# Expert weights split into two parts on GpSimd during the batches instead of in the closing stage

## The reference: what is computed

```
x = x + tanh(g_xattn) * attention(layernorm(x), ctx, ctx, Wq, bq, Wk, bk, Wv, bv, Wo, bo)   # 16 heads of 32
probs = softmax(layernorm(x) @ router_w + router_b)                                        # 8 experts
gate, idx = max(probs), argmax(probs)
x = x + tanh(g_ffn) * gate * (layernorm(x) @ expert_w[idx] + expert_b[idx])
```

## Time and profile before

| what | value |
|---|---|
| timed runs, us | 1054.35, 1055.9, 1056.93 (median 1055.9) |
| the profiled execution: its time / its span | 1057.68 / 1056.0 us |
| busy: TensorE, ScalarE, VectorE, GpSimd | 978.0, 811.9, 745.6, 262.0 us |
| mean granted TensorE clock | 0.976 of full speed |
| HBM read, written | 50.42 MB, 18.66 MB |

### The profile page before, as it was taken

How to read it: one execution, slowest core, us unless ns; L and a number is a source line. 1 busy time by engine, 2 the same in 40 slices (tenths; PEclk the granted TensorE clock), 3 DMA queues, 4 the chain that set the end, 5 groups by cost and what they waited for, 6 DMA issues and landing times.

```text
span 1056.0 us, 18686 instructions
## 1 busy us (share of the span) xinstructions
PE 978.0 (93%) x5208; PEld 641.8 (61%) x5208; DVE 745.6 (71%) x1653; ACT 811.9 (77%) x1913; POOL 262.0 (25%) x318
## 2 busy tenths in 40 slices
PE   3798999999999999999999999999999997698996
PEld 2564467656765676567656765676567545576775
DVE  5745655875787578757875787578757778797664
ACT  3688988898889888978898889888988988233431
POOL 6002200430042004200420042004201006454663
PEclk9799999999999999999999999999999989799999
DMA  6334223532443245324532453244325259144542
GB/s 213 97 90 114 79 64 98 143 85 69 115 137 89 69 110 140 89 60 117 136 81 70 117 137 84 68 116 137 86 69 132 62 166 378 56 135 137 163 138 75
DMA packets 70884, 119.37 MB, mean 113 GB/s; under 512 B 17854, under 2 KB 18878, under 8 KB 70656
## 3 DMA queue, kind: packets, MB, share of 16 engines
q1 hardware_dynamic: 64544, 99.49, 34.0%
q0 software_dynamic: 6240, 18.68, 5.5%
HBM read 50.42 MB, written 18.66 MB: 65 GB/s over the span
## 4 chain that ended last, share of the span: by engine, by line
PE 69%; ACT 10%; DVE 7%; issue 6%; DMA 3%; POOL 2%; SPq 2%; DVEq 1%; ACTq 0%; POOLq 0%
PE jb L489 11%; PE jb L490 10%; PE jb L491 10%; PE jb L532 10%; PE sc L512 9%; PE hb L522 9%; PE sc L673 6%; ACT jb L707 5%; ACT probs L695 3%; DVE maxima L819 1%; DVE e_lo L836 1%; PE hb L659 1%; PE jb L603 1%; SPq L452 1%; DMA q_stack<-q_lo 1%
## 5 line engine op out<-in xcount | busy, mean ns | idle before, releaser
L819 DVE TENSOR_REDUCE maxima<-jb 128x1 f32<-128x512 f32 x512 | 335.7, 686 | 112.0 <-PE jb L532 109.5
L707 ACT ACTIVATE jb<-jb,maxima 128x512 f32<-128x512 f32 x512 | 341.9, 678 | 41.4 <-DVE maxima L819 38.0
L695 ACT ACTIVATE probs<-sc 128x512 f32<-128x512 f32 x512 | 284.4, 605 | 40.7 <-PE sc L512 29.2
L532 PE MATMUL jb<-k_stack,q_stack 96*128 96x512 f32 x512 | 207.6, 434 | 24.4 <-ACT jb L707 10.1
L512 PE MATMUL sc<-q_stack,k_stack 98*128 98x512 f32 x512 | 183.9, 423 | 2.8 <-ACT probs L695 1.8
L532 PEld LDWEIGHTS jb<-k_stack,q_stack 96*128 96x128 f32 x512 | 95.9, 191 | 109.1 <-ACT jb L707 59.1
L522 PE MATMUL hb<-probs,values 128*32 128x512 f32 x1024 | 138.8, 616 | 1.0 <-ACT probs L695 0.7
L512 PEld LDWEIGHTS sc<-q_stack,k_stack 98*128 98x128 f32 x512 | 94.1, 191 | 67.9 <-ACT probs L695 36.6
L707 ACT ACTIVATION_READ_ACCUMULATOR jb<-jb,maxima 128x1 f32 x512 | 113.2, 221 | 0.0
L1104 POOL TENSOR_TENSOR stage<-stage,gbo 128x512 f32<-128x512 f32 x31 | 39.8, 1284 | 253.8 <-DMA stage<-in_x 253.8
L1096 POOL TENSOR_TENSOR row<-rt,tiny 128x2 f32<-128x2 f32 x15 | 12.7, 848 | 259.5 <-DVE rt L901 259.5
(11 more groups left out here) (228 smaller groups left out, 1740.3 us busy)
## 6 DMA issues: line engine op xcount, KB each, us to landing
k_stack<-k_hi SPq DMA_DIRECT2D x256, 64.0 KB, 2.0
q_stack<-q_hi SPq DMA_DIRECT2D x256, 64.0 KB, 2.0
stage<-in_x SPq DMA_DIRECT2D x63, 256.0 KB, 3.0
stage<-in_ctx_t SPq DMA_DIRECT2D x32, 256.0 KB, 3.2
k_stack<-k_lo SPq DMA_DIRECT2D x128, 64.0 KB, 2.0
q_stack<-q_lo SPq DMA_DIRECT2D x128, 64.0 KB, 2.0
e_lo<-in_ew SPq DMA_DIRECT2D x8, 1024.0 KB, 10.8
rows<-row SPq DMA_DIRECT2D x30, 257.5 KB, 3.4
```

The costliest lines, as they stand in the source:

```text
L532: nc.tensor.matmul(jbs[j][:], q_stack[g % 2][0:MAXROW, n * P:(n + 1) * P], k_stack[g % 2][0:MAXROW, h * S:(h + 1) * S], start=True, stop=T ...
L695: nc.scalar.activation(probs[:, kt % 2, h, :], scs[(16 * g + n) % NSC][:], ACT.Exp)\
L707: nc.scalar.activation(jbs[j][:], jbs[j][:], ACT.Exp, bias=maxima[g % 2][:, n:n + 1], accum_out=row_sums[g % 2][:, n:n + 1]).then_inc(s["m ...
L819: nc.vector.tensor_reduce(maxima[g % 2][:, n:n + 1], jbs[j][:], AX.X, ALU.max, negate=True)\
```

## The change

Each of the 32 chunks (an expert's 128 x 512 rows) is loaded, split and stored during batches 0 to 6 by GpSimd, five chunks a batch, through two pairs of buffers in `late_room`, a tile that is otherwise used only in the opening and at the end. Both parts are kept in two DRAM tensors. At the end SyncE loads low parts (W) and high parts (H) finished; the ScalarE, VectorE and GpSimd items W are gone.

```diff
+    ew_parts = [nc.dram_tensor(f"ew_{part}", [E, P, NF, D], F32, kind="Internal").ap() for part in ("hi", "lo")]
...
+        x_raw, x_hi = ([late_room[:, (2 * i + m) * S:(2 * i + m + 1) * S] for i in range(2)] for m in range(2))
...
# GpSimd, PER_BATCH = 5, CHUNKS = 32
+                elif kind == "XL":
+                    i = PER_BATCH * t + n
+                    if i < CHUNKS:
+                        if i < 2:
+                            wait(pool, s["w_lo_done"], 3 * NF)
+                        wait(pool, x_out[i % 2], 32 * (i // 2))
+                        nc.gpsimd.dma_start(x_raw[i % 2], ew[i // NF, i % NF * P:(i % NF + 1) * P, :]).then_inc(x_in[i % 2], 16)
+                elif kind == "XS":
...
+                        pool.wait_ge(x_in[i % 2], 16 * (i // 2 + 1))
+                        nc.gpsimd.tensor_copy(x_hi[i % 2].bitcast(F32R), x_raw[i % 2]).then_inc(s["x_hi"], 1)
+                        pool.wait_ge(s["x_hi"], i + 1)
+                        nc.gpsimd.tensor_tensor(x_raw[i % 2].bitcast(F32R), x_raw[i % 2], x_hi[i % 2], ALU.subtract)\
+                            .then_inc(s["x_lo"], 1)
+                elif kind == "XO":
...
+                        pool.wait_ge(s["x_lo"], i + 1)
+                        nc.gpsimd.dma_start(ew_parts[0][i // NF, :, i % NF, :], x_hi[i % 2]).then_inc(x_out[i % 2], 16)
+                        nc.gpsimd.dma_start(ew_parts[1][i // NF, :, i % NF, :], x_raw[i % 2]).then_inc(x_out[i % 2], 16)
# SyncE: W takes the finished low part; H is new, with the waits that ScalarE's W had
                 elif kind == "W":
...
+                    for i in range(2):
+                        wait(sp, x_out[i], 32 * len(range(i, CHUNKS, 2)))
+                    sp.dma_start(e_lo[:, n, :, :].bitcast(F32), ew_parts[1][n]).then_inc(s["ew_in"], 16)
+                elif kind == "H":
...
+                    if n in (0, 1):
+                        wait(sp, s["q_mm"], NG * B)
+                    elif n in (2, 3):
+                        wait(sp, s["st_done"], 16 * (NG * B - 1))
+                        if n == 3:
+                            sp.wait_ge(s["early_ready"], 1)
+                    elif n in (4, 5):
+                        wait(sp, s["st_done"], 16 * NG * B)
...
+                    else:
+                        wait(sp, s["pv_done"], NT * NG * B)
+                    sp.dma_start(e_hi[:, n, :, :].bitcast(F32), ew_parts[0][n]).then_inc(s["ew_in"], 16)
# TensorE, Y of tile 0
-                        wait(pe, s["ew_lo"], E)
+                        pe.wait_ge(s["ew_in"], 32 * E)
```

All order lists and the table of PSUM banks are new. The parts that matter most here:

```diff
# ORDER, POOL
-        "C3 ~~OP2 ~~OP3 LX0 LX1 LX2 LX3 ~OP0 ~~LR1 ~OP1 ~LR0 ^C0 ^C1 ^C2",
+        "C3 ~~OP2 ~~OP3 LX0 LX1 LX2 LX3 ~~LR1 ~OP0 XL0 ~OP1 XS0 XL1 XS1 XO0 XO1 XL2 XS2 XO2 XL4 XL3 XS3 XS4 XO4 ~LR0 XO3 ^C0",
+        "^C1 ^C2",
# ORDER, SP, its end
-        "^0SQ2 ^0SK2 ^0SQ3 ^0SK3 ^0MD DR1",
+        "^0SQ2 ^0SK2 ^0SQ3 ^0SK3 DR1 ^0MD",
# LAST, SP, its end
-        "3SQ0 3SQ1 3SQ2 2MD 3SK1 ~RW1 ~RW0 3SQ3 3SK2 3SK3 3MD",
+        "1SQ0 1SK0 1SK1 1SQ3 ~DR2 1SQ1 1SQ2 ~~RW2 1SK2 1SK3 ~~RW3 2SQ2 ~DR3 2SQ1 2SK0 2SQ0 2SK2 1MD 2SK1 2SQ3 DR0 2SK3 W0 W1",
+        "W2 3SQ0 3SK0 ~RW0 3SK1 3SQ1 W3 3SK2 3SQ2 2MD W4 3SQ3 3SK3 ~RW1 W5 W6 W7 3MD H0 H1 H6 H2",
# LAST, PE, its end
-        "2S10 3MT ~RL1 2S11 2S12 2S13 2S14 ~RC1 2S15 3S0 3S1 2P2 2P3 3S2 3S3 ~LI1 3S4 3S5 3S6 3S7 3P0 3S8 3S9 3S10 3S11 3P1",
-        "3P2 3S12 3S13 3S14 3S15 SA 3P3",
+        "~RL1 2S10 2S11 2P1 2S12 2S13 2S14 ~RC1 2S15 2P2 3S0 3S1 3S2 2P3 3S3 3S4 ~LI1 3S5 3S6 3S7 3P0 3S8 3S9 3S10 3P1 3S11",
+        "3S12 3S13 3S14 3S15 3P2 3P3 SA",
# LAST, ACT, its end
-        "~RT3 3MT 2E8 2E9 2E10 2E11 2E12 2E13 2E14 ~RS1 2E15 3E0 3E1 2NM 3E2 3E3 3E4 3E5 3E6 3E7 3E8 3E9 3E10 3E11 W0 3E12",
-        "3E13 3E14 3E15 W1 3NM W6 W3 W2 W4 NE0 W5 RT0 RT1 W7",
+        "3E14 3E15 3NM NE0 RT0 RT1",
# CLOSING, SP
-        "~DR2 W3 W0 ~~RW3 W1 W6 ~~RW2 ~DR1 ~DR3 W2 W4 W5 W7 EB ~RW0 ~RW1 ~RW3 ~RW2",
+        "~DR2 ~~RW2 ~DR1 ~DR3 ~~RW3 H3 H4 H5 H7 EB ~RW0 ~RW1 ~RW2 ~RW3",
# CLOSING, PE, its beginning
-        "~OP0 ~OPb0 ~OPc0 ~OPd0 ~OP2 ~OP1 ~OP3 ~OPb3 ~OPb2 ~OPb1 ~OPc1 ~OPd1 ~OPc2 ~OPc3 ~OPd2 ~OPd3 TO0 ~RT0 ~RT1 ~RT2 ~RL0",
-        "~RT3 TO1 TO2 Y0 TO3 Y1 TO4 Y2 Y3 TO5 ~RC0 Y4 ~RL1 TO6 Y5 ~LI0 TO7 Y6 TO8 Y7 TO9 Y8 ~RC1 TO10 Y9 TO11 Y10 TO12 ~LI1",
+        "~OP0 ~OP1 ~OPb1 ~OPb0 ~OPc0 ~OPd0 ~OPc1 ~OPd1 ~OP2 ~OPb2 ~OPc2 ~RT0 ~RT1 TO0 ~OP3 ~RL0 ~OPb3 ~OPd2 ~OPc3 ~OPd3 ~RC0",
+        "~RT2 TO1 Y0 TO2 Y1 TO3 Y2 TO4 ~RT3 Y3 TO5 Y4 TO6 Y5 ~RL1 ~LI0 TO7 Y6 TO8 Y7 TO9 Y8 ~RC1 TO10 Y9 TO11 Y10 TO12 ~LI1",
# CLOSING, DVE and POOL, their beginnings
-        "~OP2 ~OP3 W3 LO0 W7 LO1 LO2 ~RS0 ~RG0 FI0 LO3 LO4 FI1 ~LR2 ~LR3 FI2 FI3 LO5 ~RC0 LO6 FI4 LO7 FI5 FI6 LO8 ~LI0 ~RS1",
+        "LO0 ~RS0 ~OP2 ~OP3 LO1 ~RC0 LO2 ~LR2 ~LR3 LO3 FI0 LO4 FI1 LO5 ~RG0 FI2 LO6 FI3 FI4 FI5 LO7 ~RS1 LO8 FI6 FI7 ~LI0",
-        "~~LR1 ~OP0 ~OP1 GA0 GA2 GA3 GA5 ~OP2 GA4 ~OP3 GA1 W4 W5 ~LR0 GA6 SE0 GA7 GA9 SE1 SE3 GA8 SE2 SE4 GA10 ~LR1 GA12",
+        "~OP0 ~~LR1 GA0 GA2 ~OP1 ~OP2 GA1 ~LR0 GA3 ~OP3 GA4 GA5 GA6 GA7 GA8 SE0 ~LR1 GA9 SE3 GA10 GA11 GA12 SE4 SE6 SE1 SE2",
```

More of the change, by code:

```diff
@@ L74 @@
     "SP": [
-        "^DC0 ^DC1 ^DC2 LW1 LC ^DC3 ^DX0 LW0 ^DX1 ^DX2 LW2 ^DX3 ^0SK1 ^0SK0 LW3 ^0SK3 ^0SK2 ^0SQ0 ^0SQ1 ^0SQ2 ^0SQ3 ^0MD",
+        "^DC0 ^DC1 ^DC2 LW1 ^DC3 LC ^DX0 ^DX1 ^DX2 LW0 ^DX3 LW2 LW3 ^0SK2 ^0SK1 ^0SK0 ^0SQ0 ^0SQ1 ^0SQ2 ^0SQ3 ^0SK3 ^0MD",
     ],
     "PE": [
[4 rows of a table removed]
[4 rows of a table added]
     ],
     "ACT": [
[4 rows of a table removed]
[4 rows of a table added]
     ],
     "DVE": [
[3 rows of a table removed]
[3 rows of a table added]
     ],
@@ L100 @@
     "SP": [
-        "1SQ1 1SK0 1SQ0 1SQ3 1SK1 ~~RW3 1SQ2 ~~RW2 ~DR2 1SK2 1SK3 ~DR3 2SQ0 2SQ1 2SK0 2SK2 2SK1 DR0 2SK3 1MD 2SQ2 2SQ3 3SK0",
-        "3SQ0 3SQ1 3SQ2 2MD 3SK1 ~RW1 ~RW0 3SQ3 3SK2 3SK3 3MD",
+        "1SQ0 1SK0 1SK1 1SQ3 ~DR2 1SQ1 1SQ2 ~~RW2 1SK2 1SK3 ~~RW3 2SQ2 ~DR3 2SQ1 2SK0 2SQ0 2SK2 1MD 2SK1 2SQ3 DR0 2SK3 W0 W1",
+        "W2 3SQ0 3SK0 ~RW0 3SK1 3SQ1 W3 3SK2 3SQ2 2MD W4 3SQ3 3SK3 ~RW1 W5 W6 W7 3MD H0 H1 H6 H2",
     ],
     "PE": [
[6 rows of a table removed]
[6 rows of a table added]
     ],
     "ACT": [
[5 rows of a table removed]
[5 rows of a table added]
     ],
     "DVE": [
[3 rows of a table removed]
[3 rows of a table added]
     ],
     "POOL": [
-        "C3 ~~OP2 ~~OP3 LX0 LX1 LX2 LX3 ~~LR1 ~OP0 ~OP1 ~OP2 ~LR0 ~OP3",
+        "C3 ~~OP2 ~~OP3 LX0 LX1 LX2 LX3 ~OP0 ~~LR1 ~OP1 ~OP2 ~OP3 ~LR0",
     ],
@@ L160 @@
 BANK_TABLE = [
-    "012310231031031031201203120103210320301301",
-    "3201321301203102310231023102031201230120310213023012012012012301201231301201202013213",
-    "21032021031031231201320132013213210021032023102310213201303210310310310321031032021023023020231031",
-    "03210203213213010320132013201301302230213231023120321302101320120120120132012013032031031030312012",
-    "01320301321321020130213021302102103310321312031230132103202130230230230213023021013012012010123023",
-    "02130102132132032012301230123023021102130103210312013021323012312312312301231230201203203202031231",
-    "23012023013013213203120312031231230023012021302103201230131203103103103120310312320321321323210310",
-    "31203231201201301321032103210310312231203230123021320312010321021021021032102103132130130131302102",
-    "10321310320320320321021302132132132121231012301230130123",
-    "012302012310230",
+    "012312301201201201320132132210310321320120",
+    "1320132110320310231023102310321032013203121023103021021021023102102132302102121201320",
+    "13021302331310230231203120310310321201201023102301213201303021321321321032132130102013213232312031",
+    "20132013002021301302310231021021032312312130213012320312010132032032032103203201213120320303023102",
+    "31203120113132012013021302132132103023023201320123031023121203103103103210310312320230130101031203",
+    "12301230221213023021032103213213201031031302130231012031232301201201201320120123130312012020210321",
+    "03120312330301231230213021301301320210210123012310203210313120320320320132032031012102302323203120",
+    "31023102113130210213201320130130123203203021302103231203101023123123123012312310302031231212132013",
+    "20312031232103103012301230123023023032031203203201321320",
+    "132013010231023",
 ]
@@ L177 @@
 STEPS = {f"{k}{p}": (k, i) for k in ("Q", "K", "V", "OP") for i, p in enumerate(("", "b", "c", "d"))}
-UNBOUND = {"W", "EB", "PA", "SA", "PC", "PB", "SB", "PD", "GA", "NE", "TO", "HI", "LO", "Y", "FI", "SE"}
+UNBOUND = {"W", "H", "EB", "PA", "SA", "PC", "PB", "SB", "PD", "GA", "NE", "TO", "HI", "LO", "Y", "FI", "SE"}
 START = {"LW", "LC", "WT", "TH", "CS"}
@@ L182 @@
 NSLOT = 3
+CHUNKS = E * NF
+PER_BATCH = 5
 NHEADS = 6
@@ L402, in build @@
             "rc_mm", "rc_chain", "rc_free", "li_ready", "li_mm", "li_done", "row_out0", "row_out1",
-            "ew_lo", "eb_in", "late_in", "early_chain", "early_pick", "early_mm", "early_ready",
```

(61 more changed lines are left out.)

4 lines of the change are left out of this document (2 added, 2 removed), and 111 rows, old and new, of tables (CLOSING, LAST, OPENING, ORDER).

## The result

| | before | after |
|---|---|---|
| median of the runs | 1056.4 us (1054.4 to 1058.0, 4 runs) | 1067.4 us (1062.6 to 1070.0, 4 runs) |
| ratio, 95% interval | | 1.010 (1.006 to 1.014) |
| profiled execution, span | 1056.0 us | 1060.9 us, the fastest of its runs |

The changed kernel is slower by 1.0%. Forecast was 1043.3 us with a range up to 1056. The same comparison in later runs (e4) gave 1.014 (1.011 to 1.017).

What follows compares the result with a forecast made beforehand. TensorE was taken as busy nearly everywhere, except a hole before tile 0 filled by splits and DMA. 1057.7 - 13.1 (closing) + 0.5 (batches) = 1045.1, less 1.8 for the runs' median: 1043.3 us, range 1034 to 1056.

Steps and rivals of the forecast that it cites:

- The hole between last P and tile 0: Closing: without splits there, tile 0 starts at 896.2 instead of 909.3 us, a gain of 13.1.
- The path that ends last: Closing: of TensorE's, weights' and gather's paths to tile 0 (893, 894.8, 896.2 us), the gather's decides.
- After tile 0 nothing changes in kind: Expert tiles: the 39 tiles keep their 126 us of work and 6 us of idling.
- Doubling the weights' bytes at 0: Last batch and closing: loading 16.8 MB instead of 8.4 fits by 3 us; cost 0, bounds 0 and 8.
- GpSimd's chain: Batches: chunk loads, splits and stores ahead of LR0 take 35.3 us at 1.0 per DMA issue, leaving 4.4 spare.
- rival B: Batches: GpSimd's chain overruns its 39.7 us window and LR0 comes late; slower, 1064 us; chance 0.14.
- The failed step: Batches: 3.9 MB more traffic a batch fits the bandwidth; the added work costs 0.5 us over all seven.
- Orders at 0 with 4 to either side: Opening and batches: the new instruction orders gain or lose nothing, 0 us, bounds 4 either way.
- The rivals: Slower by GpSimd's chain (0.14), half the gain by DMA (0.15), more gain by clock and TensorE's path (0.15).
- SBUF: two separate sides: VectorE and GpSimd lock a shared port pair; by this rule GpSimd's DMA issues in batches stay near 1.0 us.

Runs made afterwards that it cites:

- e4: The changed kernel itself, unaltered, run again for its spread: 1071.4 us, ratio to the kernel before 1.0136.
- e3: Changed kernel with the old lists in opening and batches, no chunk work, weights loaded unsplit: 1051.9 us, ratio to the kernel before 0.995.
- e2: Changed kernel with its own new lists but no chunk work, weights loaded unsplit: 1054.9 us, ratio to the kernel before 0.997.
- e8: e1 with GpSimd's chunk transfers gated into the two stretches of a batch without stack transfers: 1053.6 us, ratio to the kernel before 0.9970.
- e14: e8 run a third time, as reference for e13 on its chip: 1054.8 us, ratio to the kernel before 0.9967.
- e5: e1 without the chunk transfers, GpSimd's casts and subtractions kept, weights loaded unsplit: 1053.0 us, ratio to the kernel before 0.995.
- e13: e8 with the old last-batch and closing lists on TensorE, ScalarE, VectorE and GpSimd, SyncE's new: 1075.1 us, ratio to the kernel before 1.016.
- e10: e8 with each gate opening one step later, beside stack transfers, and OP1 moved ahead: 1126.6 us, ratio to the kernel before 1.052.
- e1: Changed kernel with the old lists in opening and batches, chunk work kept: 1070.5 us, ratio to the kernel before 1.0126.
- e6: e1 without casts and subtractions, chunk transfers kept, weights loaded unsplit: 1077.9 us, ratio to the kernel before 1.019.

## Why the prediction was wrong, step by step

By medians on one chip the change adds up as follows. The closing and the last batch gave 5.2 us (e3 against before) where 13.1 were forecast. The new orders of the batches cost 3.0 (e2 less e3) where nothing was forecast. The chunk work cost 16.5 (e4 less e2) where 0.5 was forecast. Together that is 14.3 us slower (e4) instead of 12.6 faster.

- **The hole between last P and tile 0: right.** Forecast "some 18 us after the last P instead of 30.5": 17.0 in the changed kernel and 19.0 in e4, the same kernel again; 19.0 to 20.9 in e3, e8 and e14. No split is left there. The path that ends last is the gather's, as worked out; but GA0 was held by the row store and not by the plan, and GA1 landed at 908.5, 15.0 us after the last P, where I had 16.3.
- **"After tile 0 nothing changes in kind": too good by 3.7 us, and by about 6 in e3 and e4.** Idle time of 5.4 us between the tiles became 8.4 (10.0 and 9.2 in e3 and e4); attention's last items, which used to run in the hole, now stand between tiles. This is the second term that was mis-sized: of the 13.1 us forecast, 9.8 arrived in the profiled execution, which is the changed kernel's fastest, and some 5 by the medians of e3 and e5, kernels with the new closing and without the chunk transfers.
- **Doubling the weights' bytes at 0: right in size** in the changed kernel. The last weight landed at 908.8, before tile 0. e13 shows how thin that was: with another list TensorE waited 10.35 us for one MD, more than the "up to 8" of the bounds, and the last P came 17.4 us later.
- **GpSimd's chain: the working was beside the point.** A plain DMA issue took 0.54 to 0.64 us (one took 0.82), near the lower bound of 0.58 and not 1.0. Landings were 3.5 and 3.1. OP1 came 38.6 us ahead of LR0 (476.24 and 514.89), where I had about 41. LR0 was not late; it still waited 3.81 us for VectorE. So rival B's mechanism did not occur in the changed kernel. It did in e10, where LR1 was 10 us late.
- **The failed step: "Traffic grows by 3.9 MB a batch, 37 GB/s on 103 where 385 are possible ... I count 0.5 us for all seven batches."** It measured 14.7 us in the profiled executions, and 16.5 us by medians (e4 less e2). I priced bandwidth, averaged over a batch; the price was latency. The earlier trace rows say DMA share 0.39, which looks like room, but TensorE's M passes wait for the landing of small transfers that were 1.44 us each, and nothing lies between landing and use: in e1 and e3 the M began 0.1 us after its last part had landed. What the runs showed in the term's place is a wait for late stack transfers (e1 to e8), and in e1, behind the long waits, stretches at half clock, which the prediction did not count for the batches either. In the last batch I did ask what a stack DMA behind a weight load costs; in the seven batches, where it happens every time, I did not.
- **Orders at 0 with 4 to either side: right.** They lost 0.9 us (e4 less e1) and 3.0 (e2 less e3), seen in part as waits for MD (7.1 us in e2, 1.2 in e3).
- **The rivals.** None was what happened. B had its time about right (1064) for a cause that did not occur.

The Trainium skill's "DMA: Bandwidth & Descriptors", section "Issuing engines are not separate DMA queues", says that transfers of SyncE, ScalarE and GpSimd run on the same 16 DMA engines and interleave, whoever started them; its section "Queues, rings and completion order" adds that each engine takes turns between queues a whole packet at a time. e1, e6 and e8 agree with the first: transfers issued by GpSimd delayed SyncE's from 2.0 us to as much as 4.0, and stopped doing so when they were issued at another time. No run here tests the turns. For the rule of the Trainium skill's "SBUF — State Buffer", section "SBUF: two separate sides", on which the prediction leaned, the kernel before has the 11.48 us against 2.29. In the batches nothing of it is seen: the maxima took 686 ns before and after, and e5 with all the arithmetic was within 1.1 us of e3.

Left open: of the 14.7 us of the profiled executions, 12.1 are idle time of TensorE and 2.6 are longer busy time. M's waits under "issue" grew by 7.2 us, and S's for MD by 3.7, of which e2 says that they belong to the orders; M's waits for ScalarE fell by 4.5. The rest of the idle time was not followed. Nor do the runs say where on its way a stack transfer is held when chunks move beside it. And why the tiles' stretch idles 8.8 us with the new lists and 6.1 with the old was not followed to one item.

## To carry to other kernels

A free engine and a DMA share of 0.4 don't make a background transfer free: look for the small transfers for which the busiest engine waits at once, and ask how much later each lands when a 256 KB transfer runs beside it. If the background work can wait, gate it on the semaphores of those small transfers: here the same 25 MB cost 18.6 us ungated and 2 to 4 gated. And price a hole with what lies behind it: work that ran unseen in the hole comes back between the items that follow.

The gated kernel (e8) is the fastest complete version: 1.1 to 1.7% under the changed one by the ratios, and 0.1 to 0.3% under the kernel before, which is at the edge of what can be told.
